# A layer of recurrence, experts, attention and experts: four other batches through the blocks, weights before rows, and results added one stage later

## The reference

```python
x = x + rwkv(_layernorm(x), ...)          # recurrence with token mixing
x = x + ffn(_layernorm(x), router_w, w1, w2)
x = x + attention(_layernorm(x), ...)     # 16 heads of 8 channels, amplitude and phase scores
x = x + ffn(_layernorm(x), router_w, w1, w2)

def ffn(x, router_w, w1, w2):             # 8 experts, 2 for each token
    logits = tokens @ router_w.T
    topv, topi = jax.lax.top_k(logits, 2)
    w = jax.nn.softmax(topv, axis=-1)
    gate = zeros.at[arange(T)[:, None], topi].add(w)
    for e in range(8):
        h = jax.nn.gelu(tokens @ w1[e].T, approximate=False)
        out = out + gate[:, e:e + 1] * (h @ w2[e].T)
```

## Time and profile before

| what | us |
|---|---|
| median of 3 runs | 1163.03 (1160.23 to 1164.21) |
| the profiled execution | 1163.2 |
| its span, first to last instruction | 1161.4 |
| PE busy | 992.4 (85%) |
| DVE busy | 741.8 (64%) |
| ACT busy | 567.2 (49%) |
| POOL busy | 414.4 (36%) |
| mean granted TensorE clock | 0.920 of 2.4 GHz |

### The profile page before, as it was taken

The page is one execution under the profiler, slowest core; times in us unless marked ns, Lnnn a source line. Parts: engine busy times, 40 slices in busy tenths (PEclk is TensorE's granted clock), DMA queues, the critical chain, the costliest instruction groups (busy, mean ns, idle before and its releaser), DMA issues. The chain is left out here.

```text
span 1161.4 us, 17822 instructions
## 1 busy us (share of the span) xinstructions
PE 992.4 (85%) x5902; PEld 649.8 (56%) x5902; DVE 741.8 (64%) x1797; ACT 567.2 (49%) x1025; POOL 414.4 (36%) x454
## 2 busy tenths in 40 slices
PE   4888898996899768677789998999999998997885
PEld 1223233332798758534465655656666656996775
DVE  3778988996765121468786888777687654762114
ACT  1233444443653213277676766656665664542221
POOL 1455546653156054313111222222132221461543
PEclk9789978998999889888798999889899999998998
DMA  9950000000011333348788788686777600013443
GB/s 346 296 166 1 0 0 0 1 1 0 2 35 40 111 115 111 96 125 285 221 235 210 204 200 222 174 210 171 196 167 209 142 2 1 23 42 104 128 142 131
DMA packets 70918, 141.23 MB, mean 122 GB/s; under 512 B 12010, under 2 KB 38385, under 8 KB 69040
## 3 DMA queue, kind: packets, MB, share of 16 engines
q1 hardware_dynamic: 64176, 131.14, 40.8%
q0 software_dynamic: 4608, 8.47, 2.2%
q10 hardware_dynamic: 2048, 0.53, 0.2%
HBM read 82.09 MB, written 63.11 MB: 125 GB/s over the span
## 5 line engine op out<-in xcount | busy, mean ns | idle before, releaser
L1778 POOL TENSOR_SCALAR_AFFINE_SELECT attn_probs<-attn_probs 128x512 f32<-128x512 f32 x128 | 87.7, 720 | 289.3 <-ACT attn_probs L1596 289.3
L1860 DVE TENSOR_REDUCE attn_maxima<-attn_ps_p 128x1 f32<-128x512 f32 (+3 forms) x235 | 145.7, 636 | 59.0 <-PE attn_ps_p L1343 54.4
L2467 DVE SCALAR_TENSOR_TENSOR x_rows<-moe_ps_y,moe_gates,x_rows 128x128 f32<-128x128 f32 x256 | 72.0, 343 | 114.3 <-PE moe_ps_y L2245 114.1
L2318 ACT ACTIVATE moe_hidden<-moe_ps_h 128x512 f32<-128x512 f32 x168 | 91.3, 596 | 108.8 <-PE moe_ps_y L2245 108.5
L1338 PE MATMUL attn_ps_p<-attn_stack 96*128 96x384 f32 (+3 forms) x341 | 116.5, 383 | 7.9 <-DVE attn_maxima L1860 7.8
L920 POOL TENSOR_TENSOR rwkv_rs<-rwkv_recept,rwkv_state 128x512 f32<-128x512 f32 x64 | 75.9, 1186 | 108.5 <-DVE rwkv_state L1002 105.9
L1386 PE MATMUL attn_ps_q<-attn_stack 128*128 128x128 f32 (+3 forms) x343 | 106.6, 374 | 5.2 <-DMA attn_stack<-attn_neg_max 3.5
L2369 POOL DMA_INDIRECT expert_results<-moe_weighed,moe_blocked x80 | 78.4, 979 | 87.1 <-DVE moe_weighed L2457 66.7
L1002 DVE TENSOR_TENSOR_SCAN rwkv_state<-rwkv_decay,rwkv_kv 128x512 f32<-128x512 f32 x64 | 91.5, 1429 | 3.2
L1860 DVE TENSOR_REDUCE attn_maxima<-attn_ps_t 128x1 f32<-128x384 f32 (+3 forms) x117 | 74.4, 635 | 29.4 <-PE attn_ps_t L1343 27.9
L1411 PE MATMUL attn_ps_o<-attn_probs,attn_v_ones 128*32 128x512 f32 (+3 forms) x1024 | 85.2, 452 | 0.6 <-POOL attn_probs L1778 0.6
(11 more groups left out here) (317 smaller groups left out, 2177.2 us busy)
## 6 DMA issues: line engine op xcount, KB each, us to landing
attn_kept<-parts SPq DMA_DIRECT2D x32, 768.0 KB, 4.6
attn_stack<-attn_kept SPq DMA_DIRECT2D x128, 192.0 KB
moe_buffer<-in_pad SPq DMA_DIRECT2D x2, 8320.0 KB, 49.8
attn_stack<-attn_kept SPq DMA_DIRECT2D x128, 96.0 KB
value<-attn_values SPq DMA_DIRECT2D x35, 256.0 KB, 4.7
moe_blocked<-moe_buffer SPq DMA_DIRECT2D x80, 65.0 KB, 2.0
moe_w_of<-experts_in_w SPq DMA_DIRECT2D x40, 128.0 KB, 2.0
moe_w_of<-value SPq DMA_DIRECT2D x40, 128.0 KB, 2.0
```

Source lines behind the costliest of these rows:

```text
L1778: nc.gpsimd.affine_select(out=tile, in_=tile, compare_op=ALU.is_ge, fill=0.0, base=0, pattern=[[0, 4], [1, P]], channel_multiplier=-1).the ...
L1860: nc.vector.tensor_reduce(maxima[:, u % 2, h:h + heads, t], tiles, AX_X, ALU.max).then_inc(g_free, 1)
L2318: fn(hidden[:, u % 2, k * T:(k + 1) * T], ps_h[u % 2][k][:], ACT.Gelu).then_inc(gelu_done, 1)
L2467: last = stt(x[:, at:at + P], ps_y[u % 2][:, t * C:(t + 1) * C], gates[:, j, t, e:e + 1], x[:, at:at + P], ALU.mult, ALU.add)
```

## The change

- The routed batches are 2, 5, 6 and 7 (`PAIRS`), no longer 3, 4, 5 and 6. The dense ones are 0, 3, 4 and 1, which are those that the attention takes first.
- 25 dense units stand ahead of the first sparse one and two behind the last group of three (`SEQUENCE`).
- The dense batches' statistics stand in loops 2, 6 and 13 (before 2, 9 and 17), and POOL makes their 1/sqrt behind sends 4 and 24 (before 8 and 24; sends count from 0).
- SP issues the weights of the first 16 blocks as soon as the table is ready, and only then waits for the scatters; their rows come last. From block 16 on it issues four weights, then four rows. The rows wait for `unit_taken` of the unit that used the slot, no longer for `returned`.
- To make that possible DVE copies the ids of four blocks out of `blocked` into `ids_of` ahead of each sparse unit's multiplication, and POOL scatters by `ids_of`.
- The fetch of the results and the additions are a class of their own, `Results`. In moe0 they no longer stand at the end of the stage: SP issues the fetch as its first work in the attention, and DVE adds batch 5 in turn n = 1, batch 6 in n = 2, batches 7 and 2 in n = 3. The tile `combined` shares its memory with the attention's `v_ones`. In moe1 they stay at the end, with the additions in the order 5, 6, 7, 2.
- The norm of the attention's first batch is made by POOL behind the second `give_back` (before: ahead of the first), with its statistics in loop 30 (before 26).
- PE's routing of a dense batch waits for one more semaphore, since it shares a PSUM bank with the pairs' logits.

```diff
-SPARSE, DENSE = (3, 4, 5, 6), (0, 1, 2, 7)
-DENSE_AT = {1: 2, 2: 9, 3: 17}
+PAIRS, DENSE = (2, 5, 6, 7), (0, 3, 4, 1)
+PAIRS_ADDED = (1, 2, 3, 0)
+DENSE_AT = {1: 2, 2: 6, 3: 13}
-SCALED_BEHIND = {2: 8, 3: 24}
-FOLLOWING_AT = 26
-SEQUENCE = "D" * 24 + "SSD" * 5 + "DDD"
+SCALED_BEHIND = {2: 4, 3: 24}
+FOLLOWING_AT, FOLLOWING_BEHIND = 30, 1
+SEQUENCE = "D" * 25 + "SSD" * 5 + "DD"
...
+class Results:
+    def fetch(self, sp):
+        for n in range(BLOCKS - SLOTS, BLOCKS):
+            sp.wait_ge(*self.dispatch.returned_by(self.round_before, n))
+        for i, b in enumerate(PAIRS):
+            source = self.dispatch.results[b * 2 * T:(b + 1) * 2 * T].rearrange("(t p k) c -> p t (k c)", p=P, k=2)
+            sp.dma_start(self.combined[:, i], source).then_inc(self.dispatch.fetched[i], 16)
+
+    def add(self, v, i):
+        v.wait_ge(self.dispatch.fetched[i], 16 * (self.round_before + 1))
...
+        self.nc.vector.tensor_tensor(one, one, two, ALU.add).then_inc(self.added, 1)
+        v.wait_ge(self.added, earlier + 1)
+        self.nc.vector.tensor_tensor(rows_of, rows_of, one, ALU.add).then_inc(self.added, 1)
+        v.wait_ge(self.added, earlier + 2)
...
@@ attention_stage
             clear_released(nc, sp)
+            results.fetch(sp)
...
             for n in range(NB):
                 if n + 2 < NB:
                     norm.scale(v, n + 2, (turned, n + 2), FIRST[n + 2])
+                for i in [PAIRS.index(b) for b in FIRST[n + 3:8 if n == 3 else n + 4] if b in PAIRS and n < 4]:
+                    results.add(v, i)
                 if n + 3 < NB:
                     norm.statistics(v, n + 3, FIRST[n + 3])
...
@@ mixed_phase, SP
+            for n in range(SLOTS):
+                fetch_weights(n)
             for r in range(2):
                 sp.wait_ge(pairs.scattered[r], pairs.sent_in_all)
-            for n in range(BLOCKS):
+            for n in range(SLOTS):
+                fetch_rows(n)
+            for n in range(SLOTS, BLOCKS):
...
-                if n >= SLOTS:
-                    if n % GROUP == 0:
-                        sp.wait_ge(up_done, HC * (AT[(n - SLOTS) // GROUP] + 1))
-                    sp.wait_ge(*returned_by(n - SLOTS))
+                if n % GROUP == 0:
+                    sp.wait_ge(up_done, HC * (AT[(n - SLOTS) // GROUP] + 1))
+                    for m in range(n, n + GROUP):
+                        fetch_weights(m)
+                    sp.wait_ge(unit_taken, AT[(n - SLOTS) // GROUP] + 1)
+                fetch_rows(n)
...
@@ mixed_phase, PE
+                    if c in DENSE_AT and DENSE_AT[c] + 4 > PAIR_TURN[2 * r + 1] + 1:
+                        pe.wait_ge(pairs.logits_kept, r + 1)
...
@@ mixed_phase, POOL
-                    to = blocked[:, n % SLOTS, ID].bitcast(U32)
-                    pool.indirect_dma_start(results, bass.IndirectOffsetOnAxis(ap=to, axis=0), weighed[:, n % SLOTS, :], None,
+                    pool.indirect_dma_start(dispatch.results, bass.IndirectOffsetOnAxis(ap=ids_of[:, n:n + 1], axis=0), weighed[:, n % SLOTS, :], None,
...
@@ mixed_phase, DVE
+                    nc.vector.tensor_copy(ids_of[:, GROUP * i:GROUP * (i + 1)], blocked[:, at:at + GROUP, C].bitcast(U32))
...
             weigh(NU - 1)
-            for i in range(NS):
-                add(i)
+            if output is not None:
+                for i in PAIRS_ADDED:
+                    results.add(v, i)
```

More of the change, by code:

```diff
@@ L184, in __init__ @@
         self.returned = [ctx.enter_context(nc.semaphore(f"returned{s}")) for s in range(SLOTS)]
+        self.fetched = [ctx.enter_context(nc.semaphore(f"fetched{i}")) for i in range(len(PAIRS))]
         self.results = dram("expert_results", (2 * NT * P, C))
@@ L416, in find @@
         v.wait_ge(self.find_order, 2 * r + 1)
-        for t in range(PAIR):
+        for t in range(PT_):
             last = self.nc.vector.max_index(self.found[:, t, :], self.top[:, t, :], self.logits[:, t, :])
@@ L454, in rank @@
         pe.wait_ge(self.marked, 2 * r + 1)
-        mm, flat, width = self.nc.tensor.matmul, self.marks[:, r].rearrange("p t e -> p (t e)"), PAIR * NE
+        mm, flat, width = self.nc.tensor.matmul, self.marks[:, r].rearrange("p t e -> p (t e)"), PT_ * NE
         mm(to[:, 0:width], self.strict_b[:], flat[:, NE:NE + width], start=True, stop=False)
-        for t in range(PAIR):
-            last = mm(to[:, t * NE:width], self.ones_b[:], flat[:, 0:width - t * NE], start=False, stop=(t == PAIR - 1))
+        for t in range(PT_):
+            last = mm(to[:, t * NE:width], self.ones_b[:], flat[:, 0:width - t * NE], start=False, stop=(t == PT_ - 1))
         last.then_inc(self.ranked, 1)
@@ L2008, in _, with mixed_phase @@
             add_output(LAST)
-def mixed_phase(nc, phase, rows, loads, norm, pairs, table, dispatch, round_before, ready=None, following=None, output=None):
+def mixed_phase(nc, phase, rows, loads, norm, pairs, table, dispatch, results, round_before, ready=None, following=None, output=None):
     x, ident = rows.x, rows.ident
-    results, returned = dispatch.results, dispatch.returned
     HT = HC * T
@@ L2376, in _ @@
             pairs.scale_on_pool(pool, 1)
-            for n in range(4 * PAIR):
-                send(n)
+            for n in range(4 * PT_):
+                pairs.send(pool, n)
                 for c in SCALED_BEHIND:
@@ L2570, in program @@
             table = BlockTable(nc, until_experts, "moe0", pairs)
-            mixed_phase(nc, "moe0", rows, experts, first_norm, pairs, table, dispatch, 0, following=attention_norm)
+            mixed_phase(nc, "moe0", rows, experts, first_norm, pairs, table, dispatch, results, 0, following=attention_norm)
         soft = ctx.enter_context(nc.sbuf_tensor("soft", [P, 2 * T], F32))
```

153 lines of the change are left out of this document (79 added, 74 removed).

## The result

The changed kernel takes 1113.4 us (median of 4 runs, 1112.12 to 1119.66), against 1162.01 for the kernel before beside it. The ratio is 0.9592, with a 95% interval of 0.955 to 0.9633. The forecast was 1112. The profiled execution took 1112.12, its span is 1110.4 us.

A forecast was written before the change was run, and what follows sets the result against it. PE was taken to be bound by stops for blocks' rows and weights, slow clock behind them, and stage ends. From 1163.2 us, -31.5 - 4.2 + 4.3 - 25.0 + 4.0 + 1.2 = -51.2 gave 1112.0; range 1104 to 1130.

The forecast's parts named there:

- The sends: POOL's 32 sends: norm waits fall from 7.5 and 4.2 us to 0.5 and 0; last starts at 364.7.
- The sparse part: PE behind unit 20 runs through, 0.6 us of waits a stage; moe0 31.5 us less, moe1 25.0.
- the first stop: PE's wait for rows and weights before the first transposes: claimed gone, with 7 us in hand.
- The rival of SP's queue: SP's 11.4 us a cycle against PE's 11.1 bounds the sparse part: 7.5 us more a stage, 1127; chance 0.2.
- The start of the attention: Between moe0 and attention: starts at E + 6.1 instead of E + 10.3, 4.2 us won.
- E: PE's end in an expert stage, forecast at 448.1 us in moe0 and 1124.0 in moe1.
- The additions: Four deferred additions of 1.42 us on DVE in the attention: first free, other three cost 4.3 us.
- The tail: End of moe1: span ends at E + 16.4 instead of E + 12.35, 4.0 us lost.
- The rest of the attention: Attention from its first scores on PE to its end: no change forecast, 0 us.
- The range: Total time between 1104 and 1130 us; the forecast's own range 1105 to 1119.
- The rule that was weighed: DMA engines alternate between queues, so weights fetched during scatters lengthen landings: 1.0 us, last landing 368, sum unchanged.

The follow-up runs named there:

- norms_late: Changed kernel with the dense batches' statistics back in loops 2, 9, 17 and their norms behind sends 8 and 24: 1121.2 us.
- weights_behind: Changed kernel with the first 16 blocks' weights fetched behind the scatters again, in pairs with their rows: 1121.7 us.
- rows_returned: Changed kernel in which a slot's rows wait for the returned scatter again and POOL reads ids from the slot: 1141.9 us.
- norms_and_weights: Changed kernel with both the dense batches' norms in their old places and the first weights behind the scatters again: 1127.3 us.
- norm_early: Changed kernel with the attention's first norm ahead of all results' scatters, its statistics in loop 22: 1114.9 us.
- early_23_4: norm_early with 23 dense units ahead of the sparse ones and four behind the last group: 1099.5 us.
- added_at_end: Changed kernel with moe0's result fetch and four additions back at the end of moe0: 1121.6 us.
- copies_first: Changed kernel with DVE copying projections out of PSUM before additions and statistics in attention turns 2 and 3: 1117.5 us.
- after_again: The changed kernel unaltered, run again on a slower chip: 1199.2 us, ratio 0.9844 to the kernel before.
- the last set: Third set of four runs, on a slower chip, changed kernel and variants beside the kernel before, which took 1217.5 us there.

## Why the prediction was right, and where it was not

**The sends, right.** Waits at the norms 0 and 0 (forecast 0.5 and 0), at the second pair's indices 3.09 (2), last send at 364.26 (364.7), PE at the first transposes at 378.70 (379.0), no wait. What the forecast didn't see is that the change does this twice over: norms_late and weights_behind show that, with the 25th unit, either half would have done.

**The sparse part, right.** Stages 30.3 and 24.6 us shorter, with 0.5 us of waits where I took 0.6 a stage. The largest part of it is the earlier release of the slots (rows_returned, 27.7 us in both stages), then the first stop (norms_and_weights, 13.0). These make 40.7 of 54.9 us; the 14 us left, and what of them is the 25th unit, are not taken apart. The rival of SP's queue didn't come: SP never made PE wait more than 0.46 us.

**The start of the attention, wrong.** The step that failed reads "The barrier takes POOL in, so the attention starts at E + 6.1 instead of E + 10.3: 4.2 us won." POOL's own end was forecast at E+5.8 and came at E+4.7. But behind POOL's last scatter the drain runs for another 6 us, and the start came at E+10.96, 0.7 us later than before. The term for the drain was left out of the sum. It could have been seen: POOL's queue has a row of 11.4 us in the kernel before, hidden there behind DVE. norm_early moved it and early_23_4 hid it again.

**The additions, right.** +3.6 (forecast 4.3), by added_at_end 4.1. The first one waits for no fetch and is free, as forecast: DVE's idle time behind it fell from 4.11 to 2.62 us. The other three cost because DVE is full, wherever they stand in those turns (copies_first).

**The tail, right** but for 0.9 us: +4.95 against +4.0, since POOL's last scatter starts at E+0.7 and not at E.

**The rest of the attention, luck.** -4.8 us where nothing was forecast. The instructions there are the same in the ten profiles of the table, and took 403.7 to 416.0 us in them, and 411.5 for the changed kernel itself in after_again. The kernel before has four stretches of low clock behind 600 us, the one after two. One of each (columns as in the earlier trace rows):

```profile
626.00:634.00 8.00, 7.28 (x32) 5.17 (x36) 5.44 (x9) 4.48 (x9) 2.84 (x4) 0.58 0.95 221
```

```profile
600.00:608.00 8.00, 7.38 (x37) 5.01 (x37) 4.80 (x9) 3.84 (x8) 2.85 (x4) 0.57 0.97 221
```

Summed over the rest of the attention in windows of 2 us, length times (1 - granted clock) is 23.9 us before and 17.1 after. Over the ten profiles it goes from 11.9 us, where that part took 403.7, to 27.3, where it took 415.2. So an agreement to 1.4 us in the total proves little: the drain was hidden in the sum by a lucky execution, one of the changed kernel's own four runs took 1119.66, and two variants with stages as long as its own had medians of 1121 and 1122. The range held them all.

**The rule that was weighed.** Sends that landed while block weights were fetched took 2.3 to 3.4 us, median 2.6; in the kernel before from 340 to 364 us, without weights beside them, 2.3 to 2.6, median 2.4. That agrees with the Trainium skill, "DMA: Bandwidth & Descriptors", section "Queues, rings and completion order", at 0.2 us in the median. The longest says nothing: both kernels have a landing of 3.4 us among the sends from 326 to 333 us too, where no block weights are fetched. It changes nothing, as forecast.

## What to carry to other kernels

Before you move work away from the end of a block, list what every engine does in the barrier there, drains included: what was hidden behind the moved work becomes the end. Where PE is to be kept full, release a buffer when its last reader in the pipeline is done, and copy the few numbers that a later step needs; that was worth more here than any reordering. And where two edits attack one wait, undo each alone and both together, since each may hold the whole gain.

## What the hardware showed unexpectedly

- POOL's drain behind indirect scatters ended 5.9 to 6.0 us behind the last scatter's end in moe0 of all four profiles read for it (before 484.0 against 478.0, after 459.4 against 453.5, norm_early 458.3 against 452.4, early_23_4 449.7 against 443.8). after_again on the slower chip has the same 6.19 us between POOL's last scatter and its first instruction of the attention.
- The same kernel took 1113 us in the first measurement and 1199 on the chip of the last set, 86 us more; the kernel before 1162 and 1217, 55 more. The kernel that keeps PE fuller lost more; with two kernels that is no rule.
- Low clock in the attention comes at other places in each execution, with PE 7.4 of 8 us busy and a granted clock of 0.57 in the stretch shown, a mixture of 1.2 and 2.4 GHz. The rest of the attention differs by as much as 12.3 us with it.
